# Linear-attention layer with a quantised feed-forward: the old state leaves TensorE's products and is added by VectorE

## The chip, the cores and the metric

The kernel runs on one core of a Trainium2 chip. The time is the device time of one execution in microseconds (us). The engines are TensorE (PE: matmuls, and PEld: its weight loads), VectorE (DVE), ScalarE (ACT), GpSimd (POOL) and SyncE (SP, which issues the DMAs). They run at the same time and wait for one another on semaphores; each works through its own list of instructions in order.

## The reference

The input x has 2 sequences of 4096 tokens with 512 channels. The first part is a linear-attention layer (16 heads of 32) with low-rank gates, and its core is a recurrence on a 32x32 state S per head:

```python
def step(s, inp):
    q_, w_, k_, v_, a_, b_ = inp
    sa = jnp.einsum('bhij,bhj->bhi', s, a_)
    s = s * w_[:, :, None, :] + sa[..., None] * b_[:, :, None, :] + v_[..., None] * k_[:, :, None, :]
    return (s, jnp.einsum('bhij,bhj->bhi', s, q_))
_, y = jax.lax.scan(step, s0, (qt, wt, kt, vt, at, bt))
```

Before it stand a layer norm and the projections that give q (from r), w, k, v, a and b; behind it a norm per head, a bonus term, a gate, the product with Wo and the residual. The second part is a layer norm, a quantisation of each row to int8, a product with an int8 weight, scale, bias and residual. All is float32 but the quantised product.

## The kernel before

The 4096 tokens are cut into 64 tiles of 64 tokens, for both sequences at once, so that a tile has 128 rows. Three tiles are in work at a time: in step i, `mix` and `project` work on tiles i+1 and i (norm, token shift, projections, gates), `solve` on m = i-1 (the recurrence) and `finish` on n = i-2 (head norm, output product, feed-forward). Each engine has its own `tile_step`, where the order of its work is written out by hand.

The recurrence runs in chunks of 32 tokens, so NC = 2 chunks per tile. Channels lie on partitions, four heads of 32 in 128 partitions, and GS = 8 blocks hold the 16 heads of both sequences. Inside a chunk the recurrence is turned into products and one triangular solve; the inverse comes from `power` 0 to 2, `half_inverse` and `inverse`. Then each chunk c goes through this chain, of which chunk 1 needs the state of chunk 0:

- the state is multiplied by the chunk's decay and, for TensorE, laid out twice with one head of each pair set to zero (`decayed_state`, result `s_old2`): by GpSimd for chunk 0 (L438), by VectorE for chunk 1 (L902). Its signal is `sold`
- `from_values` (L1228) and `from_state` (L1240) on TensorE add into one bank of PSUM per chunk (bank_b for 0, bank_a for 1). Each block has four parts of 32 columns there: RHS (right hand side), OUT (output), NEW (new state) and SOL. `from_state` multiplies s_old2 with `aq`, whose three parts of 32 columns are the removal directions, the queries and an identity matrix: the identity columns carry the old state, decayed, into NEW. It is 16 products per chunk, which the hardware runs as 32 instructions
- `right_hand_sides` (L894, its transpose is L896) on VectorE, `solve_step` (L1248, products at L1253) on TensorE, `solution` on ScalarE (`u2`), `from_solutions` (L1257, products at L1263) on TensorE, which adds to OUT and NEW
- `update_state` (L898): VectorE transposes NEW out of the bank (L900) into `state[1]` or `state[0]` and signals `v_state`. On this signal wait `decayed_state` of the next chunk, and ScalarE's `outputs`, which copies OUT to y_sb

Around it in the queues: VectorE goes from `right_hand_sides` of chunk 0 through `bonus_sums`, `residual` (sum and its statistics), `update_state` of chunk 0, `decayed_state` of chunk 1, `mixed_inputs` for xm_wa (L779), `quantiser` (x2n at L952, a maximum at L954, two small steps and a reciprocal at L958) to `right_hand_sides` of chunk 1. GpSimd goes from `norm2_rstd` (L449, the reciprocal root of the variance that the quantiser needs) to `residual_bias` (L453: x2b = residual + bias, L399), then to its sums xm_wa to xm_rg (also L399). TensorE goes from `from_state` 0 through `output_gate`, `solve_step` 0, `gate_hidden`, `from_solutions` 0, `mixed_inputs` (L1123), `from_values` 1, `from_state` 1 to `solve_step` 1. At a tile's start TensorE's `scores_b` (L1187) waits for ScalarE's `removal_pairs` (bt, doubled by parity into a spare tile that the profile calls w_ffn_int), which follows `outputs` in ScalarE's queue.

`plast` holds the decay of each chunk, `parity` the two zero-one columns that pick a head of a pair.

Of the kernel before, what the change touches and what calls it, by code (L numbers as in the profile page):

```python
# [12 lines left out]
P = 128  # L13
# [21 lines left out]
def rwkv_ffn_kernel(nc, a, out):  # L35
# [11 lines left out]
    with ExitStack() as ctx:  # L47
        def sb(name, shape, dt=F32):
            return ctx.enter_context(nc.sbuf_tensor(name, shape, dt))

        def sem(name):
            return ctx.enter_context(nc.semaphore(name))
# [29 lines left out]
        gn_eps = sb("gn_eps", [P, 1])  # L82
        ss_shift = sb("ss_shift", [P, 1])
        sig_floor = sb("sig_floor", [P, 1])
        parity = sb("parity", [P, 2])


        xin = sb("xin", [P, C])
# [21 lines left out]
        kss = sb("kss", [P, G])  # L110
        r_raw = sb("r_raw", [P, G, CHUNK])
        val = sb("val", [P, W])
        aq = sb("aq", [P, G, 3, CHUNK])
        bt, kt = sb("bt", [P, G, CHUNK]), sb("kt", [P, G, CHUNK])


# [8 lines left out]
            spare_used[0] = hi_  # L125
            return spare[:, lo_:hi_].rearrange("p (g t) -> p g t", t=HS)

        plast = sb("plast", [P, G, 2])
        vT2 = sb("vT2", [P, G, 2, HS])
        vT = sb("vT", [P, G, HS])  # L130
        vT_raw = in_spare(G)
# [13 lines left out]
        u2 = sb("u2", [P, GS, 2, HS])  # L145
        state = [sb(f"state{n}", [P, GS, HS]) for n in range(2)]
        s_old2 = sb("s_old2", [P, GS, 2, HS])
        gate = sb("gate", [P, W])
        rkv = sb("rkv", [P, W])

# [44 lines left out]
            "pl vraw vsum vT qkT rk blT klT pm km e ptT sums te t4 tx teT t rhs state rkv".split())  # L195
        a_pw, a_u, a_y, a_g, a_b2, a_k2, a_vT2 = (sem(f"a_{n}") for n in "pw u y g b2 k2 vT2".split())
        g_qk, g_qkf, g_rkv = (sem(f"g_{n}") for n in "qk qkf rkv".split())
        sold = sem("sold")

        p_o, p_qT, p_ffn = (sem(f"p_{n}") for n in "o qT ffn".split())  # L200
        (v_ysqT, v_yvar, v_yrs, v_z1, v_yg, v_x2, v_st2, v_x2n, v_qs, v_q1, v_q2, v_ffn) = (
# [71 lines left out]
        def step_part(c, part):  # L273
            return step_bank(c)[:].rearrange("p (g j t) -> p g j t", j=4, t=CHUNK)[:, :, part, :]
# [51 lines left out]
        def _(pool):  # L326
# [40 lines left out]
            def masks():  # L367
                then(pool.memset(ident32[:], 0.0))
                for t in (mask_b, mask_k, mask_half):
                    then(pool.memset(t[:], 1.0))  # L370
                for h in range(QH):
                    q = quad(h)
                    keep(ident32[q, :], 0, 1, -1, ALU.not_equal, 1.0)
                    keep(mask_k[q, 0, :], -1, -1, 1)
                    keep(mask_k[q, 1, :], 0, -1, 1)
                    keep(mask_b[q, 0, :], -1, -1, 1)
                    keep(mask_b[q, 0, HALF:], -HALF, 1, 0)
                    keep(mask_b[q, 1, :], 0, -1, 1)
                    keep(mask_half[q, 0:HALF], HALF - 1, -1, 0)
                    keep(mask_half[q, HALF:], -HALF, 1, 0)  # L380
                nc.gpsimd.tensor_tensor(ident_half[:], ident32[:, 0:HALF], ident32[:, HALF:],
                                        ALU.add).then_inc(pool_const, 1)
                steps[0] += 1
                pool.wait_ge(pool_const, steps[0])
                nc.gpsimd.tensor_tensor(first[:, :, 1, HALF:], ident_half[:].unsqueeze(1).to_broadcast([P, G, HALF]),
                                        ident_half[:].unsqueeze(1).to_broadcast([P, G, HALF]),
                                        ALU.mult).then_inc(pool_const, 1)
                nc.gpsimd.tensor_tensor(aq[:, :, 2, :], ident32[:].unsqueeze(1).to_broadcast([P, G, HS]),
                                        ident32[:].unsqueeze(1).to_broadcast([P, G, HS]),
                                        ALU.mult).then_inc(masks_done, 1)  # L390

            def by_chunk(t):
# [2 lines left out]
            def mul(out_, in0, in1):  # L395
                return nc.gpsimd.tensor_tensor(out_, in0, in1, ALU.mult)  # L396
# [28 lines left out]
            def bonus(m):  # L425
                pool.wait_ge(v_q, count(m, 1, 1))
                mul(qk, aq[:, :, 1, :], kt[:]).then_inc(g_qk, 1)
# [10 lines left out]
            def decayed_state(m):  # L438
                pool.wait_ge(v_pl, count(m, 1, 1))
                pool.wait_ge(v_state, count(m, NC, 1))  # L440
                pl = plast[:].rearrange("p (g c) h -> p g c h", c=NC)[:, :, 0, :].unsqueeze(3).to_broadcast(
                    [P, GS, 2, HS])
                mul(s_old2[:], state[0][:].unsqueeze(2).to_broadcast([P, GS, 2, HS]), pl).then_inc(sold, 1)

            def add_bonus(n):
                pool.wait_ge(a_affine, count(n, 1, 1))
# [2 lines left out]
            def norm2_rstd(n):  # L449
                pool.wait_ge(v_st2, count(n, 3, 3))  # L450
                nc.gpsimd.tensor_tensor(rs2[:, 1:2], rs2[:, 0:1], minus_half[:], ALU.pow).then_inc(g_rs2, 1)

            def residual_bias(n):  # L453
                add(x2b[:], xres[:], ffn_bias[:]).then_inc(g_x2b, 1)
# [6 lines left out]
            def tile_step(i, mix=True, project=True, solve=True, finish=True):  # L461
                j, m, n = i + 1, i - 1, i - 2
                if mix:
                    norm_rstd(j)
                if project:
                    kept_keys(i)
                if solve:
                    decayed_state(m)
                    bonus(m)
                if finish:  # L470
                    add_bonus(n)
                if solve:
                    weighted_bonus(m)
                if project:
                    undecayed(i)
                if solve:
                    bonus_values(m)
                if finish:
                    norm2_rstd(n)
                    residual_bias(n)  # L480
                if mix:
                    mixed_inputs(j, XWA, XRG)
                if finish:
                    finish_rows(n)
# [255 lines left out]
        def _(dve):  # L740
            V = nc.vector

            def tt(out_, in0, in1, op):
                return V.tensor_tensor(out_, in0, in1, op)  # L744
# [86 lines left out]

            def enter(m):
                dve.wait_ge(a_pinv, count(m, 1, 1))
                tt(plast[:], pinv[:, :, 0:1].to_broadcast([P, G, 2]), parity[:].unsqueeze(1).to_broadcast([P, G, 2]),
                   ALU.mult).then_inc(v_pl, 1)


# [59 lines left out]

            def update_state(m, c):  # L898
                dve.wait_ge(p_s, count(m, NC, c + 1))
                V.transpose(state[(c + 1) % 2][:], step_part(c, NEW)).then_inc(v_state, 1)  # L900

            def decayed_state(m):  # L902
                dve.wait_ge(v_state, count(m, NC, 2))
                pl = plast[:].rearrange("p (g c) h -> p g c h", c=NC)[:, :, 1, :].unsqueeze(3).to_broadcast(
                    [P, GS, 2, HS])
                tt(s_old2[:], state[1][:].unsqueeze(2).to_broadcast([P, GS, 2, HS]), pl, ALU.mult).then_inc(sold, 1)

# [155 lines left out]
        def _(pe):  # L1063
# [176 lines left out]
            def from_state(m, c):  # L1240
                bank = step_bank(c)
                pe.wait_ge(sold, count(m, NC, c + 1))
                for j, g, q in step_pairs(c):
                    ins = mm(bank[q, 4 * CHUNK * j:4 * CHUNK * j + 3 * CHUNK], both(s_old2[q, j]),  # L1244
                             aq[q, g].rearrange("p j t -> p (j t)"), start=False, stop=False, skip_group_check=True)
                ins.then_inc(p_rhs, 1)

            def solve_step(m, c):  # L1248
# [163 lines left out]
```

## Time and profile before

| | before |
|---|---|
| median of 3 runs | 3243.76 us (3243.23 to 3243.87) |
| profiled execution | 3244.0 us, span 3242.2 us |
| TensorE products, busy | 3029.1 us (93%) |
| VectorE busy | 2626.5 us (81%) |
| ScalarE busy | 1974.8 us (61%) |
| GpSimd busy | 1270.6 us (39%) |
| chain that ended last | TensorE 92%, pauses for instructions ("issue") 3%, ScalarE 2%, VectorE 2% |
| granted TensorE clock, mean | 0.992 of full speed |

The span is the time from the first to the last instruction of the profiled execution; its time is 1.8 us longer. The chain that ended last is followed back from the last instruction, at each step to what released it. A line of the code can be a helper's: L744 is every `tensor_tensor` of VectorE, L399 every addition and L396 every product of GpSimd, L504 every activation of ScalarE, and the names of the tiles tell them apart.

### The profile page before, as it was taken

What the parts mean: (1) busy time and instruction counts of PE and PEld (TensorE: products, weight loads), DVE (VectorE), ACT (ScalarE), POOL (GpSimd) and SP (SyncE); (2) the same over time, 40 slices, a digit from 0 to 9 for tenths busy, and PEclk for the clock granted to TensorE, in tenths of its full rate; (3) what the DMA queues carried; (4) which work ended last, traced back from release to release, by engine and by line L of the source; (5) the groups of instructions that cost most, each with busy time, mean ns of one, the idle gap of its engine ahead of it and who ended that gap; (6) DMA issues with size and microseconds to landing.
All of it is one profiled execution on the core that took longest, in us unless ns stands there. A gap on an engine that the chain in (4) does not pass through costs nothing.

```text
span 3242.2 us, 182735 instructions
## 1 busy us (share of the span) xinstructions
PE 3029.1 (93%) x84224; PEld 2675.6 (83%) x84224; DVE 2626.5 (81%) x5443; ACT 1974.8 (61%) x3519; POOL 1270.6 (39%) x1161
## 2 busy tenths in 40 slices
PE   6999999999999999999999999999999999999996
PEld 5888888888888888888888888888888888888884
DVE  4788888888888888887888888887888878888875
ACT  3575675665665665755656656656567566566563
POOL 4334334334334344343344343443433434433332
PEclk9999999999999999999999999999999999999998
DMA  3000000000000000000000000000000000000000
GB/s 118 10 23 20 17 23 19 18 20 18 22 20 17 23 20 17 23 20 17 22 20 19 20 17 23 20 17 23 20 17 23 20 17 20 20 20 20 16 17 19
DMA packets 39380, 70.47 MB, mean 22 GB/s; under 512 B 9812, under 2 KB 10836, under 8 KB 38616
## 3 DMA queue, kind: packets, MB, share of 16 engines
q1 hardware_dynamic: 38616, 58.77, 6.8%
q8 instruction: 664, 10.88, 1.4%
q14 instruction: 100, 0.82, 0.1%
HBM read 41.97 MB, written 16.78 MB: 18 GB/s over the span
## 4 chain that ended last, share of the span: by engine, by line
PE 92%; issue 3%; ACT 2%; DVE 2%; POOL 0%; POOLq 0%; ACTq 0%; DVEq 0%
PE bank L1070 30%; PE bank_a L1209 12%; PE bank L1273 8%; PE bank_a L1187 4%; PE bank L1077 4%; PE bank_b L1187 4%; PE bank_b L1244 3%; PE bank_b L1237 3%; PE bank_a L1237 3%; PE bank_a L1244 3%; PE bank_a L1217 2%; PE bank_a L1225 2%; PE bank L1123 2%; PE bank_a L1263 2%; PE bank_b L1263 2%
## 5 line engine op out<-in xcount | busy, mean ns | idle before, releaser
L504 ACT ACT_TABLE_LOAD x383 | 491.4, 1283 | 19.1 <-DVE shift L761 12.2
L1070 PE MATMUL bank<-xm_rg,w_r 128*128 128x128 f32 x2048 | 285.4, 282 | 4.3 <-issue 3.5
L504 ACT ACTIVATE u<-bank_a,parity 128x256 f32<-128x256 f32 x128 | 53.7, 471 | 386.7 <-PE bank_a L1253 386.7
L1209 PE MATMUL bank_a<-pw,w_ffn_int 32*32 32x64 f32 x16384 | 264.6, 216 | 22.0 <-issue 17.2
L1273 PE MATMUL bank<-w_o,yc 128*128 128x512 f32 x512 | 268.9, 626 | 11.0 <-DVE yc L744 9.3
L1209 PEld LDWEIGHTS bank_a<-pw,w_ffn_int 32*32 32x32 f32 x16384 | 239.6, 106 | 41.7 <-issue 21.3
L1070 PEld LDWEIGHTS bank<-xm_rg,w_r 128*128 128x128 f32 x2048 | 248.9, 191 | 26.8 <-issue 15.9
L504 ACT ACTIVATE u<-bank_b,parity 128x256 f32<-128x256 f32 x128 | 53.8, 471 | 342.3 <-PE bank_b L1253 342.3
L1070 PEld LDWEIGHTS bank<-xm_k,w_k 128*128 128x128 f32 x2048 | 241.2, 194 | 12.5 <-issue 3.8
L1070 PE MATMUL bank<-xm_v,w_v 128*128 128x128 f32 x2048 | 250.2, 275 | 0.0
L1070 PE MATMUL bank<-xm_k,w_k 128*128 128x128 f32 x2048 | 241.7, 277 | 3.5 <-issue 3.5
L1070 PEld LDWEIGHTS bank<-xm_v,w_v 128*128 128x128 f32 x2048 | 239.3, 192 | 0.3
L870 DVE STREAM_TRANSPOSE w_ffn_int<-bank_a 128x512 f32<-128x512 f32 x192 | 137.3, 715 | 90.9 <-ACT pw L504 90.3
L399 POOL TENSOR_TENSOR yc<-yc,rkv 128x512 f32<-128x512 f32 x64 | 82.0, 1281 | 321.7 <-ACT yc L504 321.7
L396 POOL TENSOR_TENSOR kept<-ga,gma 128x512 f32<-128x512 f32 x64 | 81.5, 1274 | 311.6 <-ACT ga L504 311.6
L396 POOL TENSOR_TENSOR kkp<-kk,pinv 128x512 f32<-128x512 f32 x64 | 75.3, 1177 | 288.8 <-DVE kk L744 288.8
L396 POOL TENSOR_TENSOR kmod<-kraw,pinv 128x512 f32<-128x512 f32 x64 | 77.1, 1205 | 261.1 <-ACT pinv L504 261.1
L744 DVE TENSOR_TENSOR first<-bank_a,mask_b 128x1024 f32<-128x1024 f32 x64 | 78.4, 1225 | 106.7 <-PE bank_a L1187 106.7
L399 POOL TENSOR_TENSOR o_sb<-o_sb,x2b 128x512 f32<-128x512 f32 x64 | 81.5, 1274 | 199.3 <-DVE o_sb L968 199.3
L1209 PE MATMUL bank_a<-first,w_ffn_int 32*32 32x64 f32 x8192 | 135.0, 215 | 18.7 <-issue 17.7
L396 POOL TENSOR_TENSOR qkT<-qkT,faaaa_T 128x512 f32<-128x512 f32 x64 | 81.4, 1272 | 166.2 <-DVE qkT L914 166.2
L399 POOL TENSOR_TENSOR xm_wa<-xm_wa,xT 128x512 f32<-128x512 f32 x64 | 89.5, 1399 | 128.4 <-DVE xm_wa L779 128.4
(204 smaller groups left out, 8540.4 us busy)
## 6 DMA issues: line engine op xcount, KB each, us to landing
xin<-in_x SPq DMA_DIRECT2D x128, 128.0 KB, 2.7
xres<-in_x SPq DMA_DIRECT2D x128, 128.0 KB
out<-o_sb SPq DMA_DIRECT2D x128, 128.0 KB, 2.4
w_ffn_int<-in_weight_q SPq DMA_DIRECT2D x1, 2048.0 KB, 10.8
w_k<-in_Wk SPq DMA_DIRECT2D x1, 1024.0 KB
w_r<-in_Wr SPq DMA_DIRECT2D x1, 1024.0 KB
w_v<-in_Wv SPq DMA_DIRECT2D x1, 1024.0 KB
w_o<-in_Wo SPq DMA_DIRECT2D x1, 1024.0 KB, 14.2
```

The costliest lines, as they stand in the source:

```text
L396: return nc.gpsimd.tensor_tensor(out_, in0, in1, ALU.mult)
L399: return nc.gpsimd.tensor_tensor(out_, in0, in1, ALU.add)
L504: return nc.scalar.activation(out_, in_, func, **kw)
L870: V.transpose(pt, pairs(bank_a)[:, :, 0, :]).then_inc(v_ptT, 1)
L1070: ins = mm(bank[:, o * n:(o + 1) * n], weights[:, k, o * P:(o + 1) * P], x[:, k].rearrange("p b t -> p (b t)"), start=(k == 0), stop=(k == ...
L1077: ins = mm(bank[:, o * TOK:(o + 1) * TOK], weights[:, o * P:(o + 1) * P], hidden[:], start=True, stop=True)
L1187: ins = mm(bank[q, 64 * n:64 * n + 64], both(keys_[q, g]), both(aq[q, g, 0:2]), start=True, stop=True)
L1209: ins = mm(bank_a[q, 64 * n:64 * n + 64], pt[q, g, :], source[q, g, 0:2].rearrange("p j t -> p (j t)"), start=True, stop=True)
L1237: mm(bank[q, 4 * CHUNK * j:4 * CHUNK * j + 3 * CHUNK], both(vT2[q, g]), km[q, g].rearrange("p j t -> p (j t)"), start=(j % 4 == 0), stop=F ...
L1244: ins = mm(bank[q, 4 * CHUNK * j:4 * CHUNK * j + 3 * CHUNK], both(s_old2[q, j]), aq[q, g].rearrange("p j t -> p (j t)"), start=False, stop ...
L1263: ins = mm(bank[q, 4 * CHUNK * j + CHUNK:4 * CHUNK * j + 3 * CHUNK], both(u2[q, j]), first[q, g, 2:4].rearrange("p j t -> p (j t)"), start ...
L1273: ins = mm(fb[0][:], yc[:, k * TOK:(k + 1) * TOK], w_o[:, k, :], start=(k == 0), stop=(k == KB - 1))
```

## The change

The identity columns of `aq` go, and with them the third part of `from_state`: its products have 64 columns in place of 96. What they brought is now made by two other engines. GpSimd multiplies the old state by the chunk's decay into a new tile `carry` (`carried_state`, twice per tile): for chunk 0 right behind its `decayed_state`, for chunk 1 between `norm2_rstd` and `residual_bias`, where it waits for the new state of chunk 0. VectorE's `update_state` transposes NEW as before, then waits for that and for `carry`, adds `carry` in place, and only this addition signals `v_state`. `plast` gets a third column, the decay without parity. The product that set up the identity columns, once at the start, goes too.

```diff
-        parity = sb("parity", [P, 2])
+        parity = sb("parity", [P, 3])
-        aq = sb("aq", [P, G, 3, CHUNK])
+        aq = sb("aq", [P, G, 2, CHUNK])
-        plast = sb("plast", [P, G, 2])
+        plast = sb("plast", [P, G, 3])
+        carry = sb("carry", [P, GS, HS])
-        sold = sem("sold")
+        sold, g_carry, v_new = sem("sold"), sem("g_carry"), sem("v_new")
@@ GpSimd
-                nc.gpsimd.tensor_tensor(aq[:, :, 2, :], ident32[:].unsqueeze(1).to_broadcast([P, G, HS]),
-                                        ident32[:].unsqueeze(1).to_broadcast([P, G, HS]),
+            def carried_state(m, c):
+                pool.wait_ge(v_pl, count(m, 1, 1))
+                pool.wait_ge(v_state, count(m, NC, c + 1))
+                pl = plast[:].rearrange("p (g c) h -> p g c h", c=NC)[:, :, c, 2:3].to_broadcast([P, GS, HS])
+                mul(carry[:], state[c][:], pl).then_inc(g_carry, 1)
...
                 if solve:
                     decayed_state(m)
+                    carried_state(m, 0)
                     bonus(m)
...
                 if finish:
                     norm2_rstd(n)
+                if solve:
+                    carried_state(m, 1)
+                if finish:
                     residual_bias(n)
@@ VectorE
             def update_state(m, c):
                 dve.wait_ge(p_s, count(m, NC, c + 1))
-                V.transpose(state[(c + 1) % 2][:], step_part(c, NEW)).then_inc(v_state, 1)
+                fresh = state[(c + 1) % 2]
+                V.transpose(fresh[:], step_part(c, NEW)).then_inc(v_new, 1)
+                dve.wait_ge(v_new, count(m, NC, c + 1))
+                dve.wait_ge(g_carry, count(m, NC, c + 1))
+                tt(fresh[:], fresh[:], carry[:], ALU.add).then_inc(v_state, 1)
@@ TensorE, from_state
-                    ins = mm(bank[q, 4 * CHUNK * j:4 * CHUNK * j + 3 * CHUNK], both(s_old2[q, j]),
-                             aq[q, g].rearrange("p j t -> p (j t)"), start=False, stop=False, skip_group_check=True)
+                    ins = mm(bank[q, 4 * CHUNK * j:4 * CHUNK * j + 2 * CHUNK], both(s_old2[q, j]), both(aq[q, g]), start=False, stop=False, skip_group_check=True)
```

## Rows read from the trace of the kernel before

**Rows 1.** The page: busy time of each engine; the chain that ended last, by engine

```profile
PE 3029.1 (93%) x84224; PEld 2675.6 (83%) x84224; DVE 2626.5 (81%) x5443; ACT 1974.8 (61%) x3519; POOL 1270.6 (39%) x1161
...
PE 92%; issue 3%; ACT 2%; DVE 2%; POOL 0%; POOLq 0%; ACTq 0%; DVEq 0%
```

**Rows 2.** Chain that ended last, one tile: start us, length us, what

```profile
1501.77 1.87 PE bank_b L1187 x64
...
1529.07 1.47 PE bank_b L1244 x32
...
1533.39 1.09 PE bank_b L1263 x32
...
1537.05 1.34 PE bank_a L1244 x32
...
1539.02 0.76 PE bank_a L1253 x48
...
1539.81 0.85 ACT u L504 x2
```

**Rows 3.** Timeline of VectorE, same tile: start us, duration us, instruction, [idle before]

```profile
1534.52 0.45 DVE L900 STREAM_TRANSPOSE state<-bank_b 128x256 f32<-128x256 f32 x1 [1.19 <-PE bank_b L1263]
1535.01 0.77 DVE L744 TENSOR_TENSOR s_old<-state,plast 128x512 f32<-128x512 f32 x1
1535.69 1.11 DVE L779 SCALAR_TENSOR_TENSOR xm_wa<-bank,maa,xx 128x128 f32<-128x128 f32 x4
1536.73 0.53 DVE L952 TENSOR_SCALAR x2n<-xres,mv,rs 128x512 f32<-128x512 f32 x1
...
1538.20 0.16 DVE L958 RECIPROCAL qs<-qs 128x1 f32<-128x1 f32 x1
1538.42 0.45 DVE L896 STREAM_TRANSPOSE rhs_sb<-bank_a 128x256 f32<-128x256 f32 x1
```

**Rows 4.** Groups of VectorE, whole span: busy us, mean ns | idle us before

```profile
L900 DVE STREAM_TRANSPOSE state<-bank_b 128x256 f32<-128x256 f32 x64 | 28.8, 450 | 86.2 <-PE bank_b L1263 86.2
L896 DVE STREAM_TRANSPOSE rhs_sb<-bank_a 128x256 f32<-128x256 f32 x64 | 28.8, 450 | 5.7 <-PE bank_a L1244 1.6
```

**Rows 5.** Waits, whole span: who <- for whom: us in total, times, longest

```profile
PEld bank_b L1244 <- issue: 52.7, 73, 2.0
...
PE bank_a L1253 <- DVE rhs_sb L896: 41.2, 64, 0.6
```

**Rows 6.** Groups with 128x256 elements on VectorE and GpSimd, whole span

```profile
L744 DVE TENSOR_TENSOR first<-bank_a,mask_half 128x256 f32<-128x256 f32 x64 | 26.5, 414 | 0.0
...
L385 POOL TENSOR_TENSOR first<-ident_half 128x256 f32<-128x256 f32 x1 | 0.6, 612 | 0.1
```

**Rows 7.** Timeline of GpSimd, same tile as rows 2 and 3

```profile
1533.93 1.30 POOL L399 TENSOR_TENSOR x2b<-xres,ffn_bias 128x512 f32<-128x512 f32 x1
1536.89 1.41 POOL L399 TENSOR_TENSOR xm_wa<-xm_wa,xT 128x512 f32<-128x512 f32 x1 [1.66 <-DVE xm_wa L779]
```

**Rows 8.** Timeline of the last tile: VectorE's x2n, GpSimd's x2b

```profile
3229.85 1.50 DVE L952 TENSOR_SCALAR x2n<-xres,mv,rs 128x512 f32<-128x512 f32 x1 [0.66 <-POOL rs L451]
...
3229.78 1.29 POOL L399 TENSOR_TENSOR x2b<-xres,ffn_bias 128x512 f32<-128x512 f32 x1
```

**Rows 9.** Instructions of one tile's name: ns min/median/max, first and last start

```profile
L396 POOL TENSOR_TENSOR s_old<-state,plast x64: 1055/1057/1063, 74.8 to 3180.6; 128x512 f32<-128x512 f32 x64
...
L744 DVE TENSOR_TENSOR s_old<-state,plast x64: 691/762/774, 104.4 to 3205.4; 128x512 f32<-128x512 f32 x64
...
L399 POOL TENSOR_TENSOR xm_wa<-xm_wa,xT x64: 1171/1410/1417, 24.2 to 3116.2; 128x512 f32<-128x512 f32 x64
```

**Rows 10.** Timeline of ScalarE and TensorE at the end of the same tile

```profile
1545.97 0.38 ACT L504 ACTIVATE y_sb<-bank_a 128x256 f32<-128x256 f32 x1 [1.06 <-DVE state L900]
1546.38 1.33 ACT L504 ACTIVATE w_ffn_int<-bt,parity 128x512 f32<-128x512 f32 x2
...
1548.19 1.02 PE L1187 MATMUL bank_a<-aq,w_ffn_int 64*64 64x64 f32 x27
```

More of the change, by code:

```diff
@@ L386, in masks @@
                                         ident_half[:].unsqueeze(1).to_broadcast([P, G, HALF]),
-                                        ALU.mult).then_inc(pool_const, 1)
-                nc.gpsimd.tensor_tensor(aq[:, :, 2, :], ident32[:].unsqueeze(1).to_broadcast([P, G, HS]),
-                                        ident32[:].unsqueeze(1).to_broadcast([P, G, HS]),
                                         ALU.mult).then_inc(masks_done, 1)
@@ L440, in decayed_state @@
                 pool.wait_ge(v_state, count(m, NC, 1))
-                pl = plast[:].rearrange("p (g c) h -> p g c h", c=NC)[:, :, 0, :].unsqueeze(3).to_broadcast(
+                pl = plast[:].rearrange("p (g c) h -> p g c h", c=NC)[:, :, 0, 0:2].unsqueeze(3).to_broadcast(
                     [P, GS, 2, HS])
                 mul(s_old2[:], state[0][:].unsqueeze(2).to_broadcast([P, GS, 2, HS]), pl).then_inc(sold, 1)
+            def carried_state(m, c):
[3 more added lines that the diff above has]
+                mul(carry[:], state[c][:], pl).then_inc(g_carry, 1)
             def add_bonus(n):
@@ L833, in enter @@
                 dve.wait_ge(a_pinv, count(m, 1, 1))
-                tt(plast[:], pinv[:, :, 0:1].to_broadcast([P, G, 2]), parity[:].unsqueeze(1).to_broadcast([P, G, 2]),
+                tt(plast[:], pinv[:, :, 0:1].to_broadcast([P, G, 3]), parity[:].unsqueeze(1).to_broadcast([P, G, 3]),
                    ALU.mult).then_inc(v_pl, 1)
@@ L899, in update_state @@
                 dve.wait_ge(p_s, count(m, NC, c + 1))
-                V.transpose(state[(c + 1) % 2][:], step_part(c, NEW)).then_inc(v_state, 1)
+                fresh = state[(c + 1) % 2]
[3 more added lines that the diff above has]
+                tt(fresh[:], fresh[:], carry[:], ALU.add).then_inc(v_state, 1)
             def decayed_state(m):
                 dve.wait_ge(v_state, count(m, NC, 2))
-                pl = plast[:].rearrange("p (g c) h -> p g c h", c=NC)[:, :, 1, :].unsqueeze(3).to_broadcast(
+                pl = plast[:].rearrange("p (g c) h -> p g c h", c=NC)[:, :, 1, 0:2].unsqueeze(3).to_broadcast(
                     [P, GS, 2, HS])
```

## The prediction

> **What bounds the kernel now.** I read the page first: TensorE is busy for 93% of the span and the chain that ended last lies on it for 92% [rows 1]. So time is won only where TensorE itself gets shorter, or waits less. Then the chain of waits through one of the 64 tiles [rows 2]: it stays on TensorE from the first product with the state (1529.07) to the second one (1537.05 and 1.34 long). There it leaves TensorE for the only time but one: the second solve begins at 1539.02, behind VectorE's transpose of the right hand sides [rows 2, 3]. The other time is ScalarE's copy of the solutions (1539.81) [rows 2], which the change does not touch.
>
> So the question is what lets that transpose start at 1538.42. Its group shows 5.7 us of idle VectorE time before 64 of them, under 0.1 us each [rows 4], while the transpose of the new state (L900, bank_b) has 86.2 us before it, 1.35 us each, ended by TensorE [rows 4]. So VectorE waits for TensorE at the state and from there on runs without a pause: decayed state, mixed inputs, quantiser, reciprocal, then the transpose [rows 3]. The reciprocal ends at 1538.36; TensorE's second state product ends at 1538.39 (1537.05 + 1.34). The two arrive within 0.1 us of one another. That is what the reader is to see: TensorE gains nothing there unless VectorE arrives earlier too, and anything put on VectorE between 1534.52 and 1538.42 goes straight into TensorE's wait. VectorE's true slack: neighbours that don't depend on one another overlap by 0.07 to 0.08 us (1535.78 against 1535.69 [rows 3]), so it could have begun at 1538.28: slack 0.14.
>
> **Part 1: shorter products from the state.** 32 products per chunk go from 96 to 64 columns. Today they take 1.47 us [rows 2]. The products from the solutions have the same count, the same 64x64 weights, 64 columns, and accumulate: 1.09 us, so 0.38 gained. The scores, 64 in 1.87 us, would give 0.93 and a gain of 0.54 [rows 2]. I take 0.38, as that row also accumulates into the same banks. For chunk 0 this is on the path: all that follows comes 0.38 earlier. For chunk 1 the products are done 0.38 earlier, but the transpose behind them does not start before VectorE gets there: worth nothing. TensorE runs as many instructions as before, so its pauses for instructions ("issue") stay where they are. 52.7 us of them stand ahead of the weight loads of this very product [rows 5]; where such a pause ends at a time set by the loading of code, a quicker product in front of it only lengthens it. I guess that in about one tile in six the 0.38 is lost: 4 us, between 0 and 10.
>
> **Part 2: the addition, chunk 0.** It reads two tiles of SBUF, 128x256. VectorE's nearest row of that size takes 0.41 [rows 6], and half of the decayed state's 0.69 would be 0.35; I take 0.42, as the half of a long one leaves out the fixed part. It waits for the transpose (dependent neighbours stand 0.03 to 0.04 apart, 1534.97 to 1535.01 [rows 3]) and for GpSimd's product, which GpSimd makes early in the tile, right after its own decayed state: no wait. Together 0.45 (0.38 to 0.5). The other readers: TensorE's state product 1 needs the decayed state, now there at 1535.78, used at 1537.05 [rows 2, 3]; it comes 0.45 later, 1.3 us of cover, so nothing.
>
> **Part 3: GpSimd's product for chunk 1, and what is queued behind it.** It stands between the reciprocal root and the residual plus bias (x2b). Now x2b runs from 1533.93 to 1535.23, before and under the transpose of the state, and GpSimd then idles until 1536.89 [rows 7]. With the change GpSimd stops at a wait for the new state, and x2b, 1.30 us, is queued behind it. That matters for a reason that the rows of the last tile show: there x2b started at 3229.78 and ended at 3231.07, and VectorE's x2n, 0.53 us in a tile of the middle [rows 3], started at 3229.85 and ended at 3231.35, 1.50 us long, 0.28 after x2b's end [rows 8]. The decayed state shows it too: 0.69 at its shortest [rows 9], 0.77 where x2b still runs under its first 0.2 us, so that it ends 0.55 after x2b [rows 3, 7]. GpSimd is held the other way: xm_wa is started under x2n [rows 3, 7] and takes 1.41. Mixed inputs (from PSUM) and transposes show no such thing.
>
> The Trainium skill says so in "SBUF — State Buffer", section "SBUF: two separate sides": VectorE and GpSimd share a port pair that the first comer holds for its whole instruction, against VectorE instructions with two SBUF inputs or in a two-port mode. By that rule, the trace agrees (the 1.50 us above), x2n is held as in the sum; without it the case is rival (a).
>
> Now the schedule, in us after the end of the state's transpose (1534.97). Addition 0.03 to 0.45, GpSimd idle. Then both engines are released; VectorE's own signal takes 0.03, GpSimd starts 0.09 after VectorE (1536.80 to 1536.89 [rows 3, 7]), so VectorE goes first: decayed state 0.48 to 1.17, at its short 0.69. GpSimd's product is held to about 1.04 (xm_wa, 1.17 where nothing holds it [rows 9], ended at 1538.30, so it was freed at 1537.13, 0.13 before x2n's end) and takes 0.61, by its one row of this size [rows 6] (0.53 if half of its 128x512 row [rows 9]): to 1.65. x2b: 1.61 to 2.90. Mixed inputs on VectorE: 1.10 to 2.21. x2n would start at 2.14, finds x2b on the port until 2.90, and ends 0.28 later, at 3.18. Today it ends at 2.29 (1537.26). VectorE is 0.89 later at the transpose, less 0.14 of slack: 0.75. Should GpSimd win the port first: its product to 1.05, decayed state to 1.60, x2n unhindered to 3.10: 0.67, nearly the same. x2b also lets SyncE load the next residual; it ends 2.6 us later (1537.87 in place of 1535.23) in a tile of about 50 us (3242 over 64): nothing.
>
> **Part 4: the addition, chunk 1.** VectorE again 0.45 later from there on. The state's signal releases ScalarE's y_sb (1545.97), and behind it the doubled removal keys, done at 1547.71; TensorE's scores start at 1548.19 [rows 10]. Of these 0.48 a part is the delay from signal to start: 0.15 at the second solve (1538.87 to 1539.02 [rows 2, 3]), taken as 0.12 since a weight load goes ahead. So 0.36 is slack, and 0.45 passes it by 0.09. GpSimd's third product, for chunk 0 of the next tile, delays the bonus product by 0.6; behind it GpSimd waits for others: nothing, up to 0.1 per tile if it holds a VectorE step. The lost setup product (1 us, once) is nothing.
>
> **Sum.** Per tile: -0.38 + 0.75 + 0.09 = +0.46 us. 63 tiles have a finished tile beside their solve: +29. With 4 for lost gains at pauses, less 1 for setup: +32. The profiled execution took 3244.0 (span 3242.2), the median of the runs is 3243.76, 0.2 less, so 3276.
>
> **Rivals.** (a) *Not slower: x2n is not held.* If x2b were out of the way, or did not hold it, x2n would end at 2.67: 0.38 later, less 0.14: 0.24. Per tile -0.38 + 0.24 + 0.09 = -0.05, and with the pauses' 4 us: 3244. For it: the rows show x2n held in one tile only, the one where x2b starts ahead of it. Against: that tile's rows are plain, and x2b would have to start 0.76 earlier than it can; that is the point from which this decides. Chance 0.15.
> (b) *Faster: VectorE catches up.* Only if the transpose had a microsecond of slack: both gains count, -0.76, + 0.09, 63 times: 3201. The 5.7 us of idle time [rows 4] speak against it. Chance 0.04.
> (c) *Worse.* x2n costs its whole 0.53 after x2b (+0.25), or GpSimd's product early in the tile holds VectorE where power 1 is late (+0.1): up to +0.35 a tile, 3292 to 3298. Chance 0.11.
> (d) *The columns were not the cost*: 64 columns take as long as 96. Then 0.38 more per tile: 3296. Against: 1.09 and 1.47 for the same count. Chance 0.04.
> Forecast (x2n held, 3260 to 3290): 0.66.
>
> **Numbers.** 3276. The range reaches down to (a) and up to (c) and (d): 3243 to 3298; outside are (b), the lower part of (a), and a little above. This kernel can be told from no change from about 0.2% on, 6.5 us. Slower by more: 0.66 + 0.11 + 0.04 + a little of (a): 0.82. Within: 0.12. Faster: 0.06.
>
> **What would show it.** State products at 1.09 in place of 1.47, both chunks. The decayed state on VectorE at 0.69 always. x2n near 1.04 long, ending 0.28 after x2b, in nearly all tiles. The idle time of TensorE ahead of the second solve (41.2 us in all today [rows 5], 0.64 each) up by 1.1 us a tile: 0.38 gained in front of it and 0.75 lost. TensorE waiting for ScalarE at the scores by about 0.1. I am wrong if x2n stays at 0.53, or if the transpose of chunk 1 has idle time before it that TensorE ended.

## The result, and the profile after

The changed kernel takes 3351.97 us (median of 4 runs) where the kernel before took 3243.49 beside it (median of 4): a ratio of 1.0333, 95% interval 1.0315 to 1.0352. So it is slower, as forecast, but by about 108 us and not by 32: it lies above the whole range. Its four runs took 3334.5 to 3354.93 us; the profiled one is the slowest, 3354.93, its span 3353.2.

First the two lines that the view of the cores gives, kernel before, then kernel after (span, and mean granted clock of TensorE):

```profile
core 0: 3242.2 us, clock 0.992
core 0: 3353.2 us, clock 0.962
```

A mean clock of 0.992 means that at most 26 us (0.008 of 3242.2) were lost to the clock in all, 0.962 that at most 127 us were. In the kernel before, nearly all of it lies at the two ends: the granted clock is 0.95 in the first 100 us, 0.77 in the last 42, and 1.00 between:

```profile
100.00:3200.00 3100.00, 2945.57 (x82668) 2603.47 (x82661) 2556.73 (x5296) 1925.71 (x3432) 1220.16 (x1058) 1.00 0.07 19
```

(The stretch, its length, busy us and instructions of PE, PEld, DVE, ACT and POOL, the granted clock, DMA share and GB/s.) From 100 to 3300 us of the changed kernel it is 0.97. This is the first hint. Next the head of the page of the kernel after, which answers to [rows 1]:

```profile
PE 3063.2 (91%) x84224; PEld 2708.7 (81%) x84224; DVE 2713.6 (81%) x5571; ACT 1980.5 (59%) x3519; POOL 1369.1 (41%) x1288
PE 83%; DVE 10%; issue 3%; ACT 2%; SPq 1%; DMA 0%; POOL 0%; POOLq 0%; ACTq 0%; DVEq 0%
```

The products from the state were cut by a third, and TensorE is busy for more microseconds than before; VectorE, all but absent from the chain before, now has 10% of it. The chain of waits through the same tile as in [rows 2], kernel after (start, us, what):

```profile
1533.10 1.08 PE bank_b L1256 x32
...
1538.17 0.46 DVE state L909
1538.65 0.44 DVE state L752
1539.11 0.69 DVE s_old L752
1539.80 1.04 DVE xm_wa L787 x4
1540.84 1.00 DVE x2n L964
1541.87 0.70 DVE qs L966
...
1542.94 0.36 DVE rhs_sb L904
1543.43 0.77 PE bank_a L1264 x48
1544.22 0.85 ACT u L512 x2
1545.11 1.97 PE bank_a L1274 x32
1547.08 3.71 PE bank L1082 x16
1550.79 1.22 PE bank L1300 x4
```

Read it in two halves. The first half is what the forecast describes: the product is down to 1.08, and the chain no longer stays on TensorE but runs through VectorE from the state's transpose (L909), the addition (0.44), the decayed state, the mixed inputs and an x2n of 1.00 to the transpose of the right hand sides. The second half is not in the forecast. The products from the solutions (L1274, 32 of them) take 1.97; in the kernel before they took 1.09 for chunk 0 [rows 2] and 1.15 for chunk 1. The 16 hidden products behind them took 1.98 before and take 3.71. Nothing in the diff touches them. The view by windows says why, with the columns as above, first of the kernel before (from its second solve on), then of the kernel after:

```profile
1539.00:1546.00 7.00, 6.44 (x134) 5.72 (x135) 6.97 (x19) 3.00 (x9) 3.87 (x3) 1.00 0.01 2
```
```profile
1541.60:1543.30 1.70, 0.03 (x2) 0.00 (x0) 1.60 (x6) 0.00 (x0) 1.26 (x1) 1.00 0.00 0
1543.30:1544.50 1.20, 1.07 (x68) 0.89 (x68) 1.17 (x4) 0.28 (x1) 0.00 (x0) 1.00 0.00 0
1545.00:1552.00 7.00, 6.89 (x54) 6.04 (x55) 6.96 (x16) 2.31 (x8) 3.86 (x3) 0.54 0.01 2
1552.00:1560.00 8.00, 8.00 (x181) 7.81 (x183) 4.06 (x10) 5.11 (x8) 1.79 (x2) 1.00 0.28 67
```

From 1545 to 1552 the granted clock is 0.54, that is 1.2 GHz for nearly all of 7 us, and then 2.4 GHz again. Before, the same stretch ran at 1.00. The clock does not fall in the long wait (1541.6 to 1543.3), nor as it ends: the second solve still runs at 2.4 GHz and takes 0.77, as before (0.76). It falls about 1.2 us later, while TensorE waits for ScalarE's copy of the solutions, and the first products at 1.2 GHz are those behind that second wait.

Not every tile loses this. In the trace of the changed kernel the clock falls some 40 times between the first 130 us and the last 60, about half of them for 7 us and the others for half as long. And here are six tiles in a row, each with the same wait (10.4 us for the six, 1.73 each), without any fall:

```profile
1705.00:2001.90 296.90, 274.91 (x7868) 243.05 (x7867) 248.73 (x513) 184.79 (x328) 123.54 (x112) 1.00 0.08 20
```

So the wait makes the fall likely, but does not bring it each time. The Trainium skill says of this, in "TensorE: Matmul & The Clock Gate", section "Part 1: The HAM clock gate", that "the default state is throttled, and activity releases the throttle"; the 0.54 in a tile with the longer wait and the 1.00 without it agree, and the six tiles above show that a wait of this length alone does not decide. What the chip looks at no run here shows.

How much that is over all tiles stands in the groups by line and operation (busy us, mean ns of one | idle time before). Kernel before, then after:

```profile
L1070 PE MATMUL bank<-xm_wa,w_hwa 128*128 128x128 f32 x512 | 76.4, 294 | 5.0 <-POOL xm_wa L399 5.0
L1263 PE MATMUL bank_a<-first,u 64*64 64x64 f32 x2048 | 73.7, 221 | 35.2 <-ACT u L504 35.2
L1070 PE MATMUL bank<-xm_k,w_hk 128*128 128x128 f32 x512 | 69.8, 281 | 0.0
L1289 PE MATMUL bank<-w_ffn,qT 128*128 128x512 bf16 x256 | 66.6, 383 | 0.7 <-ACT qT L504 0.7
L1244 PE MATMUL bank_b<-aq,s_old 64*64 64x96 f32 x2048 | 106.0, 252 | 4.8 <-issue 4.5
L1244 PE MATMUL bank_a<-aq,s_old 64*64 64x96 f32 x2048 | 95.3, 243 | 0.0
```
```profile
L1082 PE MATMUL bank<-xm_wa,w_hwa 128*128 128x128 f32 x512 | 109.2, 379 | 5.0 <-POOL xm_wa L397 5.0
L1274 PE MATMUL bank_a<-first,u 64*64 64x64 f32 x2048 | 101.1, 270 | 33.4 <-ACT u L512 33.4
L1082 PE MATMUL bank<-xm_k,w_hk 128*128 128x128 f32 x512 | 88.7, 331 | 0.0
L1300 PE MATMUL bank<-w_ffn,qT 128*128 128x512 bf16 x256 | 71.4, 404 | 0.7 <-ACT qT L512 0.7
L1256 PE MATMUL bank_b<-aq,s_old 64*64 64x64 f32 x2048 | 78.9, 224 | 6.3 <-issue 5.9
L1256 PE MATMUL bank_a<-aq,s_old 64*64 64x64 f32 x2048 | 70.3, 218 | 0.8 <-DVE s_old L752 0.8
```

The first four groups, which stand behind the second solve and which the change leaves as they were, cost 32.8 + 27.4 + 18.9 + 4.8 = 83.9 us more. The products from the state cost 52.1 less. The third term is the wait, kernel after (us in all, times, longest), to be held against the 41.2 of [rows 5]:

```profile
PE bank_a L1264 <- DVE rhs_sb L904: 109.7, 64, 1.8
```

68.5 more. Together 83.9 + 68.5 - 52.1 = 100.3 of the 111 by which the spans differ; where the other 11 lie these views don't tell. Without the clock's 83.9 it would be 16, and 22 with the forecast's 0.09 a tile at the scores. (In the changed kernel that wait is not there in most tiles: its slowed products make TensorE late, so that the scores follow at once.) 22 is near the forecast's 32. That is an account, and not yet a cause: it doesn't show that the wait brings the clock down, nor that the time comes back if the clock stays up.

### The profile page after: what moved, and what is told of

It is laid out like the page before. It is cut to its first block, busy times and chain, and to the rows that moved or that the text cites. A ratio compares the mean times of both kernels' runs of the same rounds, so it can differ in the third digit from the quotient of the medians.

```text
span 3353.2 us, 183246 instructions
## 1 busy us (share of the span) xinstructions
PE 3063.2 (91%) x84224; PEld 2708.7 (81%) x84224; DVE 2713.6 (81%) x5571; ACT 1980.5 (59%) x3519; POOL 1369.1 (41%) x1288
## 4 chain that ended last, share of the span: by engine, by line
PE 83%; DVE 10%; issue 3%; ACT 2%; SPq 1%; DMA 0%; POOL 0%; POOLq 0%; ACTq 0%; DVEq 0%
PE bank L1082 30%; PE bank_a L1221 11%; PE bank L1284 7%; PE bank_a L1199 4%; PE bank L1089 4%; PE bank_b L1199 4%; PE bank_a L1274 3%; PE bank_b L1249 3%; PE bank_a L1229 2%; PE bank_a L1237 2%; PE bank_b L1256 2%; PE bank_b L1274 2%; PE bank L1164 2%; DVE xm_wa L787 2%; DVE x2n L964 2%
## 5 line engine op out<-in xcount | busy, mean ns | idle before, releaser
L1221 PE MATMUL bank_a<-pw,w_ffn_int 32*32 32x64 f32 x16384 | 263.3, 215 | 20.7 <-issue 15.6
L1264 PE MATMUL bank_a<-rhs_sb,tx 32*32 32x32 f32 x4096 | 49.8, 195 | 109.9 <-DVE rhs_sb L904 109.7
L394 POOL TENSOR_TENSOR carry<-state,plast 128x256 f32<-128x256 f32 x128 | 108.7, 849 | 101.3 <-DVE state L752 101.3
```

The costliest lines, as they stand in the source:

```text
L1221: ins = mm(bank_a[q, 64 * n:64 * n + 64], pt[q, g, :], source[q, g, 0:2].rearrange("p j t -> p (j t)"), start=True, stop=True)
```

## The experiments

The theory: GpSimd's and VectorE's work make TensorE wait 1.7 us per tile, as forecast, and a wait of that length makes products behind it run at 1.2 GHz. The rival: the missing 76 us (108 less the forecast's 32) are work or waits of the change itself, which the forecast priced too low (the port between GpSimd and VectorE, the addition, pauses of TensorE). Each ratio below is against the kernel before on the same chip; "lost to the clock" is one minus the mean granted clock, times the span, as above. The changed kernel itself was timed in the first series only, where the kernel before took 3243 us; beside the runs below it took 3229 to 3233. Where a run is held against the changed kernel, it is the two ratios that are compared.

### Is it the clock, and does the wait set it?

**The changed kernel with its wait filled.** Six extra products of 128x128 (12 instructions), whose result nobody reads, between the second products from the state and the second solve. GpSimd and VectorE are left as they are.

```
         from_state(m, 1)
+        filler(6)     # 6 x mm(bank of chunk 0, w_r, w_k)
         solve_step(m, 1)
```

> The changed kernel, and TensorE runs 12 more instructions of 128x128 (6 products, results in a part of a bank that nobody reads any more) between the second product with the state and the second solve, 1.3 us, where it now waits 1.7. Theory (the granted clock falls because of this wait, and that is the 75 us that the forecast lacks): with more work the kernel gets faster, clock back to 0.99, solutions' products of chunk 1 1.08 to the next in place of 1.5, about 3277 us, what the forecast gave. Rival (the clock falls for another reason, or the wait itself is the whole loss): 3352 or more, clock 0.96.

1.0093 (1.0063 to 1.0122), clock 0.992; some 3274 us by this ratio, where 3277 were expected. Its groups and its wait:

```profile
L1082 PE MATMUL bank<-xm_wa,w_hwa 128*128 128x128 f32 x512 | 76.0, 293 | 5.0 <-POOL xm_wa L397 5.0
L1280 PE MATMUL bank_a<-first,u 64*64 64x64 f32 x2048 | 73.5, 221 | 35.4 <-ACT u L512 35.4
L1261 PE MATMUL bank_b<-w_k,w_r 128*128 128x128 f32 x768 | 102.7, 284 | 0.0
PE bank_a L1270 <- DVE rhs_sb L904: 14.9, 58, 0.3
```

The means are back at 293 and 221, those of the kernel before. TensorE does 102.7 us of useless work and the kernel gains 2.4% on the changed one. VectorE is as late as in the changed kernel: its x2n still has a median of 1.07, and TensorE, the fillers done, still waits a little for the right hand sides in 58 tiles. So the rival is out: the change itself costs 0.93%, some 30 us. What filled the wait also took the loss away.

**The kernel before with a late VectorE.** One or two transposes into a tile that nobody reads, ahead of the second transpose of the right hand sides. Nothing of the change is in these kernels.

```
         if solve:
+            for spare_n in range(2):      # range(1) in the first
+                V.transpose(waste[:, spare_n], w_k[:, 0, :]...)
             right_hand_sides(m, 1)
```

> The kernel before, with one transpose of 128x512 that nobody reads (0.63 us) on VectorE ahead of the transpose of the right hand sides of chunk 1: a dose of waiting for TensorE, with nothing else changed. TensorE's wait ahead of the second solve 0.64 + 0.63 - 0.14 = 1.13 us. If only the wait counts: +0.49 in 64 tiles, 31 us, ratio 1.010, clock 0.99. Theory of the clock (the longer this wait, the more tiles run on at 1.2 GHz; so far 28 us lost at 0.64, 35 and 43 at 0.9, 52 at 1.02, 71 at 1.43, 127 at 1.71, counted as time at the lower level times one half): about 55 to 60 lost, ratio 1.016 to 1.020, clock about 0.98.

> The same with two such transposes: wait 1.76 us, nearly that of the changed kernel (1.71), but with 96 columns, no addition and nothing new on GpSimd. If only the wait counts: +1.12 in 64 tiles, 72 us, ratio 1.022, clock 0.99. Theory of the clock: 130 us lost as in the changed kernel, 100 more than before, ratio 1.05, clock 0.96; solutions' products of chunk 1 and the products behind them at half speed in most tiles.

One: 1.0119 (1.0104 to 1.0134), wait 67.6 us, where the clock's theory had 1.016 to 1.020 and the wait alone 1.010. Its profiled run is its slowest (3289.83, clock 0.984); the other four took 3272 to 3275 at 0.987 to 0.989. So at 1.06 us a tile the clock costs little on most runs. Two: 1.0368 (1.0354 to 1.0381), clock 0.974:

```profile
PE bank_a L1256 <- DVE rhs_sb L897: 105.2, 64, 1.7
L1073 PE MATMUL bank<-xm_wa,w_hwa 128*128 128x128 f32 x512 | 102.9, 363 | 5.0 <-POOL xm_wa L400 5.0
L1266 PE MATMUL bank_a<-first,u 64*64 64x64 f32 x2048 | 95.1, 260 | 35.0 <-ACT u L505 35.0
L1073 PE MATMUL bank<-xm_k,w_hk 128*128 128x128 f32 x512 | 77.3, 301 | 0.0
L1292 PE MATMUL bank<-w_ffn,qT 128*128 128x512 bf16 x256 | 70.2, 400 | 0.7 <-ACT qT L505 0.7
```

Two wasted transposes cost 121 us. 64.0 are the wait (105.2 against 41.2), and the four groups give 26.5 + 21.4 + 7.5 + 3.6 = 59.0, together 123 (the spans of the two profiled runs differ by 114). So 1.0 us more of wait per tile costs nearly twice its length, without any part of the change. This is the mechanism by itself, but smaller than expected (1.05 and a clock of 0.96): a wait of 1.64 a tile loses 77 to 87 us to the clock in its four runs, where the changed kernel with 1.71 loses 97 to 127. What brings the rest is taken up under "Still open".

### The parts of the change

**GpSimd's products alone** (made and waited for, used by nobody; the products keep 96 columns, no addition), and **the addition alone** (adding a tile of zeros behind the transpose).

```
+    carried_state(m, 0)            # GpSimd, as in the change
     ...
+    carried_state(m, 1)            # ahead of residual_bias(n)
```
```
-    V.transpose(state[(c + 1) % 2][:], step_part(c, NEW)).then_inc(v_state, 1)
+    V.transpose(fresh[:], step_part(c, NEW)).then_inc(v_new, 1)
+    tt(fresh[:], fresh[:], carry[:], ALU.add).then_inc(v_state, 1)     # carry = 0
```

> The kernel before, with only GpSimd's part of the change: both products with the decay, in the changed kernel's places, into a tile that nobody reads; the products keep 96 columns and nothing is added. Theory (x2b, queued behind the product, holds x2n): decayed state 0.69, GpSimd's product to 1.21 us after the state's transpose, x2b to 2.46, x2n held until then and 0.28 more: 2.74 in place of 2.29, less 0.14 of slack: +0.31 per tile, 3263 us, x2n about 1.05 long, TensorE's wait ahead of the second solve 0.95. Rival (GpSimd costs nothing, all is VectorE's addition): 3243, x2n 0.53. Theory of the clock: if a wait of 0.95 is already too long, the granted clock falls below 0.99 and up to 80 us come on top.

> The kernel before, with only VectorE's part: the new state is transposed, waited for, and a tile of zeros is added to it. Theory: for chunk 0 x2b still holds the port for its first 0.23 us, so the addition ends at 0.54 and the decayed state takes 0.69: +0.50, less 0.14 of slack: 0.36; for chunk 1 0.09 at the scores: +0.45 per tile, 3272 us; wait ahead of the second solve 1.0. Rival (the whole loss of the change is the queue on GpSimd): 3243 to 3250. Theory of the clock: below 0.99 if a wait of 1.0 is too long.

GpSimd alone: 1.0105 (1.0066 to 1.0144), wait 58.0, clock 0.987 (0.985 to 0.992 in its four runs). The tile x2n in it (ns: shortest, median, longest):

```profile
L965 DVE TENSOR_SCALAR x2n<-xres,mv,rs x64: 537/1023/1505, 154.6 to 3254.7; 128x512 f32<-128x512 f32 x64
```

No instruction of VectorE is added, and yet its x2n goes from 0.53 [rows 3] to 1.02: the port, as forecast. Of some 34 us, 16.8 are the wait; the hidden products and those from the solutions take 84.7 and 79.8, which is 14.4 more for the clock.

The addition alone: 1.0129 (1.0101 to 1.0157), wait 56.8, clock 0.990. The wait's 15.6 and 8 for the clock (the same two groups, 81.3 and 76.9), with 6 at the scores, make 30 of some 42. Where the other 12 lie these views don't tell. The median from the end of the projections ahead of the scores to the start of the scores grew by 0.09 us (from -0.07, the overlap of neighbours, to 0.02), and from the doubled removal keys to the scores it shrank from 0.47 to 0.10: the slack of part 4 is used up and passed by its 0.09. The two parts add up to 2.3% and the change costs 3.3%. That they draw on the same slack, and that the clock falls more often as the wait grows, fits this, but no run takes the two apart.

**The shorter products alone.** The old state is not carried: this kernel leaves that part of the computation out.

```
-    bank[q, ... + 3 * CHUNK], both(s_old2[q, j]), aq[q, g]...   # 96 columns
+    bank[q, ... + 2 * CHUNK], both(s_old2[q, j]), both(aq[q, g])
```

> The kernel before, with only TensorE's part: the products from the state have 64 columns, and the old state is carried on by nothing (this part of the computation is left out). Theory: chunk 0 gives its 0.38; in chunk 1 the transpose can start 0.14 earlier: -0.52 per tile, 3211 us; wait ahead of the second solve 0.88, clock 0.99. Rival (TensorE's clock falls because its products became narrower): clock about 0.96 and slower than before, 3270 or more.

1.003 (1.0013 to 1.0048), where 3211 us, a ratio of 0.99, was expected: with 52 us less work on TensorE and nothing added it is not faster. Its decayed state, and GpSimd and VectorE of one tile:

```profile
L741 DVE TENSOR_TENSOR s_old<-state,plast x64: 691/1023/1043, 103.7 to 3196.9; 128x512 f32<-128x512 f32 x64
1535.37 1.29 POOL L396 TENSOR_TENSOR x2b<-xres,ffn_bias 128x512 f32<-128x512 f32 x1
1536.18 1.03 DVE L741 TENSOR_TENSOR s_old<-state,plast 128x512 f32<-128x512 f32 x1
```

The state is there sooner, so VectorE reaches the decayed state while x2b still has the port: the decayed state starts 0.48 before x2b's end (1536.66) and ends 0.55 after it, 1.03 long in place of 0.77. The gain of 0.38 is mostly given back there, the wait ahead of the second solve is 65.0, and the clock takes its part again (0.984). **Filled** in the same way (four products), which leaves out the same part:

> The third experiment (64 columns alone, the old state is not carried on) with 8 more instructions of 128x128 on TensorE ahead of the second solve, 0.9 us, where it waits 1.02. Theory (what the narrower products gain there, the clock takes back): clock 0.984 back to 0.99, ratio 1.003 down to 0.993 to 0.996. Rival (the shorter products gain nothing in any case): ratio 1.003 or more.

0.9947 (0.9934 to 0.9961), clock 0.992, no wait for the right hand sides left. TensorE's 52 us were worth 17 here, where the clock is held up. As the fillers now leave no wait at all, they may themselves hold up the solve, so 17 is a lower bound.

### Can the change be arranged so that it pays?

**x2b ahead of GpSimd's product.**

```
     norm2_rstd(n)
+    residual_bias(n)
     if solve: carried_state(m, 1)
-    residual_bias(n)
```

> The changed kernel with one swap on GpSimd: x2b goes ahead of the product for chunk 1, as x2b stands in the kernel before. Rival (a) of the forecast (with x2b out of the way x2n is not held, and the change costs nothing): x2n 0.53, 3244 us or ratio 1.00. Theory after the third experiment, in which the decayed state grew to 1.02: x2b starts when GpSimd's own queue lets it, while the state comes 0.38 earlier; so x2b now holds the addition, then ends at 0.64 us after the state's transpose: addition to 0.92, decayed state to 1.64, x2n to 3.14 in place of 2.29, which is 0.71 late after the slack of 0.14, nearly the 0.75 of the changed kernel. So x2n 0.53, addition of chunk 0 about 0.9, wait ahead of the second solve 1.6, granted clock 0.96 to 0.97, ratio 1.025 to 1.033.

1.0187 (1.0148 to 1.0227), better than the 1.025 to 1.033 that was expected. x2n is short again, and another is held:

```profile
L963 DVE TENSOR_SCALAR x2n<-xres,mv,rs x64: 533/536/1476, 154.2 to 3272.7; 128x512 f32<-128x512 f32 x64
1555.66 1.28 POOL L397 TENSOR_TENSOR x2b<-xres,ffn_bias 128x512 f32<-128x512 f32 x1
1556.47 0.76 DVE L751 TENSOR_TENSOR state<-state,carry 128x256 f32<-128x256 f32 x1
```

The addition is 0.76 long and ends 0.29 after x2b. The wait is 91.8, 1.43 a tile against 1.71: less late by 0.28, and the kernel better by 1.4%, some 47 us, where 0.28 a tile makes 18. The clock brought the rest: the four groups behind the second solve have 329.2 us (95.1 + 92.1 + 74.4 + 67.6) against 370.4 in the changed kernel, and the mean clock is 0.979 against 0.962.

**VectorE's order changed too:** x2n, but not the rest of the quantiser, ahead of the transpose of the right hand sides; the transpose of the bonus and the undecayed keys behind the second new state; on TensorE the transposes of the quantised rows behind the products from the solutions. Once in the changed kernel with x2b first, once in the kernel before.

```
-    quantiser(n)
+    normalised_rows(n)                  # x2n alone
     right_hand_sides(m, 1)
+    quantiser(n)                        # the rest
     quantised_rows(n)
```

> The changed kernel with x2b first, and the queues put in another order around it: VectorE transposes the right hand sides of chunk 1 right after x2n and does the rest of the quantiser behind it; the new state of chunk 1 is transposed and added between bt and kt, where VectorE waits for the port anyway; the bonus is transposed at the tile's end; TensorE transposes the quantised rows after the solutions' products of chunk 1. Theory (the change loses because its work lies on VectorE between the state and the second solve, and the wait it makes lowers the clock): wait ahead of the second solve back to 0.64 to 0.75, both 0.38 gained, clock 0.99: -0.6 to -0.7 per tile, ratio 0.985 to 0.99. Rival (VectorE as a whole is the bound, whatever the order): the loss turns up at the scores or at the products of the next tile instead, ratio 1.00 to 1.02.

> The kernel before with the same new order of the queues and nothing of the change: control for the run before it. Theory: TensorE already lets the transpose start on time there, so the order gives nothing: wait 0.64, ratio 0.998 to 1.002. Rival (the order alone is the gain): ratio 0.99 or less.

Changed: 1.0034 (1.0022 to 1.0046). Before: 1.0139 (1.0105 to 1.0174). Both wait 41.2 for the right hand sides, and both wait longer for ScalarE's copy of the solutions, the place from which the transposes were taken (60.0 against the 35.2 before). x2b first and the order together help the changed kernel by 2.9%, the order alone by 1.5% (1.0187 to 1.0034), and it hurts the one before; in this order the change itself is worth 1% to the good. Both expectations missed: 0.985 to 0.99 for the changed kernel, and no cost of the order for the kernel before. The rows of the kernel before in this order give 24.8 us more of the wait for the solutions, 10.8 in which TensorE's weight loads wait for GpSimd's xm_k, which now comes later, and the clock's part (the hidden products' two groups and those from the solutions take 84.1, 77.0 and 78.1 in place of 76.4, 69.8 and 73.7).

**Both waits filled,** two products ahead of the second solve and three behind it; and, as a control, the kernel before with two and two.

```
     from_state(m, 1)
+    filler(2)
     solve_step(m, 1)
+    filler(3)                           # filler(2) in the control
     from_solutions(m, 1)
```

> The changed kernel in the new order of the sixth experiment, with 4 more instructions of 128x128 on TensorE ahead of the second solve (0.45 us in a wait of 0.64) and 6 behind it (0.67 us in a wait of 0.94 for ScalarE). Theory (the new order brought the 0.76 us per tile, and the clock took most of it, since the quantised rows' transpose no longer lies in the second wait): clock 0.983 back to 0.992, ratio 1.0034 down to 0.993 to 0.996, faster than both kernels. Rival: ratio 1.003 or more.

> Control: the kernel before with 4 more instructions of 128x128 in each of its two waits. Theory (at waits of 0.64 and 0.54 the clock hardly falls in the steady tiles: 28 us lost in all, as in the filled changed kernel): ratio 0.999 to 1.003, clock 0.992. Rival (the filling helps every kernel): ratio 0.997 or less.

The changed kernel, reordered and filled: 0.9934 (0.9918 to 0.995), clock 0.993: the one kernel that computes everything and is clearly faster than both, by about 20 us and some 130. From its chain of waits in one tile:

```profile
1570.65 0.64 PE bank_b L1265 x4
...
1571.30 0.77 PE bank_a L1274 x48
...
1572.98 1.15 PE bank_a L1284 x32
```

The second solve now follows the fillers (L1265) at once, no VectorE stands in it, and the products from the solutions take 1.15. The control gives 0.9988 (0.9979 to 0.9997): filling alone is worth a tenth of a per cent to the kernel before, whose clock was hardly down. Against it the changed kernel gains about 0.5%, once its lateness is ordered away and its waits are filled. How much of that is the change and how much the order is not shown: the kernel before was not run with both the new order and the fillers.

## Why the prediction was right in direction and wrong in size

**Part 1, the products: right.** 1.08 for the forecast 1.09 in chunk 0, 1.10 in chunk 1. That chunk 1's shorter product would only lengthen the wait is right too: the wait grew by 1.07 a tile, of which 0.38 is this.

**Part 2, the addition: right.** 0.44 to 0.45 on the chain. GpSimd's product for chunk 0 is ready in time.

**Part 3, x2b and the port: right.** The rows of GpSimd and VectorE in the tile of the chain, kernel after:

```profile
1539.22 1.07 POOL L394 TENSOR_TENSOR carry<-state,plast 128x256 f32<-128x256 f32 x1 [1.34 <-DVE state L752]
1540.25 1.29 POOL L397 TENSOR_TENSOR x2b<-xres,ffn_bias 128x512 f32<-128x512 f32 x1
1540.76 1.07 DVE L964 TENSOR_SCALAR x2n<-xres,mv,rs 128x512 f32<-128x512 f32 x1
```

Counted from the end of the state's transpose (1538.62): the product ends at 1.67 (forecast 1.65), x2b starts at 1.63 (1.61), x2n ends at 3.21 (3.18). Its median over the tiles is 1.07 (forecast 1.04), and the decayed state is 0.69 in every one. The transpose of the right hand sides starts at 4.24 where it was 3.45 before [rows 3]: 0.79 later for 0.75. (The prediction reads an overlap of 0.07 to 0.08 between neighbours, where 1535.78 against 1535.69 is 0.09; that moves its slack by 0.01 and nothing else. It also says that mixed inputs are not held, for which [rows 3, 7] have no case; the kernel after has one: 1.12 us long from 1539.72 on, under GpSimd's product, against 1.11.)

**Part 4: right,** 0.09, in the kernel with the addition alone and in the filled one. In the changed kernel itself it stays hidden in most tiles, as TensorE comes late to the scores.

**The wait: right.** "Up by 1.1 us a tile": 1.71 against 0.64.

**The sum: wrong, and this is the step that failed.** "-0.38 + 0.75 + 0.09" prices a wait at its own length and lets all that comes behind it run as fast as before. It holds when the clock is kept up: 1.0093 measured for the forecast 1.0100. It left out that, with a 1.7 us wait ahead of the second solve, TensorE's clock falls to 1.2 GHz behind that solve in most tiles: +83.9 us in four groups that the change doesn't touch, 1.3 us a tile. No rival held this either; (c), the worst, ended at 3298, because it again only made the wait longer. The profile of before gave only a weak hint: its mean clock of 0.992 shows that the clock can fall, but there it falls almost only at the two ends, with TensorE less busy. The question "what runs at 1.2 GHz if this wait becomes 1.7 us" was not put. No row of before could have given its size, but half speed for the 4 us of products behind the second solve (1.15, 1.98 and 0.86) was a case that its trace allowed to be priced, at 4 us a tile.

**Rival (a)** (x2n not held) and **(d)** (columns without a price) are out by the rows above. **Rival (b)** is out for this kernel. Its core, that both gains would count if VectorE weren't late, was seen only in part: 17 of TensorE's 52 us with the products alone and the wait filled.

**Still open.** How the loss grows with the wait, and what else it hangs on. In order of the wait per tile, with the us lost to the clock over the runs of each kernel (in the profiled runs 19 to 26 of them at the two ends):

| wait us | kernel | columns | lost to the clock |
|---|---|---|---|
| 0.64 | before | 96 | 13 to 32 |
| 0.89 | addition alone | 96 | 33 to 43 |
| 0.91 | GpSimd alone | 96 | 26 to 49 |
| 1.02 | shorter products alone | 64 | 45 to 65 |
| 1.06 | one transpose | 96 | 36 to 43, once 53 |
| 1.43 | x2b first | 64 | 66 to 86 |
| 1.64 | two transposes | 96 | 77 to 87 |
| 1.71 | the change | 64 | 97 to 127 |

At like waits the kernels with the shorter products lose more: 1.02 with 64 columns more than 1.06 with 96, and 1.43 about as much as 1.64. So part of the loss may come from the narrower products themselves. No run changes the columns alone at one and the same wait, so this is not shown. And 0.64 together with a longer wait behind the solve lost 55 in the reordered kernel, and 49 in the kernel before in that order (profiled runs). So waits near one another seem to count together; the rule is not settled by these runs.

## What to carry to other kernels

On TensorE a wait can have two prices: its length, and a stretch a little behind it at half rate. Ask of each wait that a change lengthens what TensorE does in the next microseconds (here it was not the first product behind the wait but those from 1.7 us on), and price a case with those instructions at twice their time. Where the wait can't be taken away, cheap work in its place can pay: 12 useless instructions a tile took the changed kernel from 1.0333 to 1.0093, and with an order that makes VectorE less late 10 took it from 1.0034 to 0.9934.

## What the runs showed of the hardware

- A wait of 1.7 us per 50 us, with one of 0.9 us behind it, is enough to have TensorE run at 1.2 GHz for 7 us or half of that in most tiles (some 40 of 64), although it is busy for 91% of the span. In the tile shown the clock fell about 1.2 us after the long wait had ended, and six tiles in a row with the same wait kept a granted clock of 1.00.
- Useless products in the wait kept the clock up: 102.7 us of them brought the mean clock from 0.962 to 0.992 and the ratio from 1.0333 to 1.0093.
- Adding GpSimd instructions of 0.63 us, one of them ahead of x2b, slows VectorE without giving it any work: x2n from 0.53 to 1.02. An instruction that is held is counted as busy: the product of 0.63 shows as 1.07 where VectorE has the port. So a busy time on GpSimd or VectorE is no price of the work.
- A shorter instruction can lose by being early: with the products alone, the decayed state met x2b on the port and went from 0.76 to 1.02.
